# A graph-network kernel whose adjacency loads are merged from two of 2 MB to one of 4 MB

## What is computed

```python
h = relu(layernorm(x))
Wh = h @ W
e = leaky_relu(Wh @ a1 + (Wh @ a2).T, 0.2)
att = softmax(where(adj > 0, e, -9e15), axis=-1)
x = x + relu(att @ Wh)
h = relu(layernorm(x))
node = h @ W1
hw = einsum('nc,kcf->nkf', h, W2)
y = adj @ einsum('nk,nkf->nf', node, hw)
out = x + relu(y + node @ b)
```

## Time and profile before

| | |
|---|---|
| median of 3 runs | 1871.63 us (1871.55 to 1872.37) |
| profiled execution, device time | 1872.76 us |
| its span, first to last instruction | 1871.2 us |
| PE busy | 98% of the span |
| ACT, DVE, POOL busy | 71%, 65%, 38% |
| moved by DMA | 452 MB, 242 GB/s over the span |
| mean granted clock of TensorE | 0.993 of full speed |

### The profile page before, as it was taken

One profiled execution on the slowest core, in us unless ns is written; L12 is line 12 of the kernel. 1 busy time (PEld: TensorE's weight loads), 2 busy tenths in 40 slices (PEclk: granted clock), 3 DMA queues, 4 the chain that ended last, 5 costly groups with the idle time before them and its releaser, 6 DMA issues.

```text
span 1871.2 us, 38399 instructions
## 1 busy us (share of the span) xinstructions
PE 1831.2 (98%) x13404; PEld 1590.1 (85%) x13404; DVE 1209.9 (65%) x1511; ACT 1330.3 (71%) x2144; POOL 714.5 (38%) x530
## 2 busy tenths in 40 slices
PE   7799999999999999999999999999999999999998
PEld 4699989889889888988988888898877788888886
DVE  6666677677767767777776776776656543443534
ACT  4666788877878787887788778878465655555554
POOL 0300056546546655654665564565535400000000
PEclk9899999999999999999999999999999999999999
DMA  9488967776776776777777677674753344445430
GB/s 332 154 311 320 352 243 283 289 276 265 287 288 251 295 290 251 288 284 274 271 287 278 263 292 280 251 295 156 309 198 144 141 161 161 154 159 205 152 157 22
DMA packets 105812, 452.24 MB, mean 242 GB/s; under 512 B 6736, under 2 KB 15136, under 8 KB 87968
## 3 DMA queue, kind: packets, MB, share of 16 engines
q1 hardware_dynamic: 86720, 356.53, 51.2%
q10 hardware_dynamic: 12208, 75.62, 9.9%
q0 software_dynamic: 6832, 19.41, 2.8%
HBM read 364.46 MB, written 87.07 MB: 241 GB/s over the span
## 4 chain that ended last, share of the span: by engine, by line
PE 91%; DVE 3%; ACT 2%; issue 2%; SPq 1%; DMA 1%; DVEq 0%; ACTq 0%
PE ot_ps L806 47%; PE mt_ps L850 13%; PE ot_ps L850 13%; PE hw_ps L770 11%; PE mt_ps L738 6%; ACT wh_mask L505 1%; PE h_ps L765 1%; DVE att L947 1%; DMA adj_sb<-in_adj_dram 1%; SPq L283 1%; DVE p_sb L971 1%; DVE p_sb L897 1%; ACT prod L571 1%; DVE keep L952 0%; PE h_ps L777 0%
## 5 line engine op out<-in xcount | busy, mean ns | idle before, releaser
L806 PE MATMUL ot_ps<-wh_mask,p_sb 128*128 (+1 forms) x8192 | 980.6, 277 | 5.8 <-DVE p_sb L971 5.8
L971 DVE SCALAR_TENSOR_TENSOR p_sb<-zb,qcol,mt 128x1024 f32<-128x1024 uint8 (+1 forms) x512 | 780.6, 1555 | 263.3 <-ACT mt L517 212.2
L806 PEld LDWEIGHTS ot_ps<-wh_mask,p_sb 128*128 128x128 f32 x8192 | 942.3, 192 | 7.7 <-issue 5.9
L378 POOL TENSOR_TENSOR prod<-prod 128x1024 f32<-128x1024 f32 (+2 forms) x192 | 408.0, 2125 | 516.5 <-ACT prod L571 500.6
L505 ACT ACTIVATE wh_mask<-adj_sb 128x2048 uint8<-128x2048 f32 x256 | 492.9, 1928 | 3.3 <-DMA adj_sb<-in_adj_dram 2.2
L632 ACT ACTIVATE mask<-adj_sb 128x1024 fp32r<-128x1024 uint8 x240 | 255.4, 1065 | 176.5 <-PE ot_ps L850 176.4
L517 ACT ACTIVATE mt<-mt_ps 128x1024 uint16<-128x1024 uint16 x256 | 267.5, 1046 | 151.8 <-PE mt_ps L738 150.5
L1009 DVE CAST mask<-adj_sb 128x1024 fp32r<-128x1024 uint8 x272 | 202.3, 750 | 248.5 <-PE mt_ps L850 246.6
L571 ACT ACTIVATE prod<-hw_ps,node 128x128 f32<-128x128 f32 x1024 | 278.8, 385 | 92.1 <-PE hw_ps L770 92.1
L850 PE MATMUL mt_ps<-mask,msgs 128*128 128x512 f32 x1024 | 283.0, 398 | 4.3 <-issue 3.4
L850 PE MATMUL ot_ps<-mask,msgs 128*128 128x512 f32 x1024 | 275.6, 391 | 0.8
(11 more groups left out here) (112 smaller groups left out, 612.5 us busy)
## 6 DMA issues: line engine op xcount, KB each, us to landing
adj_sb<-in_adj_dram SPq DMA_DIRECT2D x128, 2048.0 KB, 8.4
maskT_d<-mt ACTq DMA_DIRECT2D x64, 1024.0 KB, 5.2
adj_sb<-maskT_d SPq DMA_DIRECT2D x32, 2048.0 KB, 7.7
keep_d<-keep POOLq DMA_DIRECT2D x64, 128.0 KB, 6.0
p_sb<-keep_d SPq DMA_DIRECT2D x4, 2048.0 KB, 12.2
msg_d<-msg POOLq DMA_DIRECT2D x56, 128.0 KB, 5.9
msgs<-msg_d SPq DMA_DIRECT2D x7, 1024.0 KB, 10.2
wh_mask<-in_x_dram SPq DMA_DIRECT2D x8, 512.0 KB, 7.3
```

The lines of the kernel that those rows point to most:

```text
L378: pool.tensor_tensor(prod[:, 0:n, :], prod[:, 0:n, :], prod[:, n:2 * n, :], ALU.add)\
L806: ins = pe.matmul(ot_ps[h][:, (t - t0) * ROW:(t - t0 + 1) * ROW], p_sb[:, r, t * P:(t + 1) * P], rows, start=False, stop=end and t == t1 - 1)
L971: dve.scalar_tensor_tensor(p_sb[:, r, :], zbf[:, bass.ds((ib % 2) * BLK, BLK)], qcol[:, bass.ds(tile + b_, 1)], mtb[:, p, k, :, b_], ALU.m ...
```

## The change

The two loads of a half turn become one. SP waits until both quarters of the half have been cast, then issues one load of all eight rows per partition (4 MB) into both quarters; it raises one semaphore, `adj_in[p]`, and all four casts of the half wait for that one. The casts, their order, `adj_cast`, and everything behind them are as before. `past_sp` is a semaphore that nothing waits for; the increment only separates two waits on SP.

```diff
--- before.py
+++ after.py
@@ -185,7 +185,7 @@
         z0_copied = sem("z0_copied")
         z_stored = sem("z_stored")
         zb_in = sem("zb_in")
-        adj_in = [sem(f"adj_in{q}") for q in range(4)]
+        adj_in = [sem("adj_in0"), sem("adj_in1")]
         adj_cast = [sem(f"adj_cast{q}") for q in range(4)]
         turned = sem("turned")
         evicted = sem("evicted")
@@ -287,12 +287,12 @@
             def turn(i, ib, jg, finish, last):
                 for p in range(2):
                     for h in range(2):
-                        q = 2 * p + h
-                        sp.wait_ge(adj_cast[q], i)
-                        sp.dma_start(adj_sb[:, q, :].rearrange("p (t n) -> p t n", n=BLK),
-                                     adj_v[bass.ds(ib, 1), :, h * HT:(h + 1) * HT,
-                                           bass.ds((2 * jg + p) * BLK, BLK)].rearrange("i p t n -> (i p) t n"))\
-                          .then_inc(adj_in[q], 16)
+                        sp.wait_ge(adj_cast[2 * p + h], i)
+                        sp.sem_inc(past_sp, 1)
+                    sp.dma_start(adj_sb[:, 2 * p:2 * p + 2, :].rearrange("p h n -> p (h n)")
+                                 .rearrange("p (t n) -> p t n", n=BLK),
+                                 adj_v[bass.ds(ib, 1), :, :, bass.ds((2 * jg + p) * BLK, BLK)]
+                                 .rearrange("i p t n -> (i p) t n")).then_inc(adj_in[p], 16)
 
             attention_loop(sp, turn)
 
@@ -499,7 +499,7 @@
 
             def cast(q, part, count, turned_before):
 
-                act.wait_ge(adj_in[q], 16 * count)
+                act.wait_ge(adj_in[q // 2], 16 * count)
                 act.wait_ge(turned, turned_before)
                 t = q % 2 * HT + part * (HT // 2)
                 ins = act.activation(m8[:, q // 2, t:t + HT // 2, :].rearrange("p t n -> p (t n)"),
```

## The result

| | before | changed |
|---|---|---|
| median | 1871.97 us (6 runs, 1871.55 to 1872.57) | 1879.12 us (6 runs, 1877.34 to 1880.01) |
| ratio to before | | 1.0037, 95% interval 1.0024 to 1.0050 |
| span of the profiled execution | 1871.2 us | 1875.8 us |

The change makes the kernel 7.15 us slower, 0.37%. The forecast was 1876.7 us, or 4.7 us above that median. The profiled execution of the changed kernel is its fastest run (1877.34 us); a second set of runs, further down, has a profile nearer to its median.

The account below looks back on a forecast made before the run. The prediction took PE to bound the kernel (busy 98% of the span, 91% of the chain). Its terms, +5.1 + 0 + 0 + 0 on the median 1871.63, gave 1876.7 us, range 1872.8 to 1883.

Parts of the forecast that it names:

- The first load: At the start, the first cast waits for all 4 MB, landing at 34.2 us in place of 29.1: +5.1 us.
- That nothing absorbs it: Behind the first cast, everything is waiting, so the 5.1 us delay arrives at the end whole.
- The clock: PE's clock behind the first wait and at the start of attention: 3.84 us won or lost as bounds, taken as 0.
- The rival by which the clock gives the delay back: At the start of attention and the step after the wait, full clock returns 3.84 us: 1872.9 us, not slower; chance 0.23.
- Loads in block 0: Attention loads in block 0 take 15.5 us of the 18.3 us available, 2.8 us to spare, so cost 0.
- the 12.5 to 16 us that the prediction named: Sign for the profile after: loads should land in 12.5 to 16 us.
- its own sign, that ACT waits for a load after 82 us: During attention, the prediction called itself wrong if ACT waits for a load after 82 us.
- the loads of attention: Loads in blocks 0 to 7 fit between issue and need: 15.5 of 18.3 us, later 16.3 of 21.5; cost 0.
- Less traffic in the way: Fewer, longer loads leave gaps for small stores; PE could win 4.3 us over blocks 1 to 7, 1868.6 us; chance 0.03.
- A late load at the end of block 0: Rival: block 0 loads over 18.3 us stall ACT, 4.9 us late at 23.2, up to 14.7 us in all; chance 0.08.

Follow-up runs that it names:

- second set of runs: The changed kernel run and profiled again, nothing altered: 1879.84 us (5 runs) against 1872.58 for the kernel before, ratio 1.0041.
- The kernel with nothing else changed: The kernel before with only the two half turns of the first turn loaded as 4 MB, other loads at 2 MB: 1877.53 us against 1872.17.
- with all of the costs of the change removed: The changed kernel with the first turn at 2 MB loads, first xt load before attention, start casts one step later: 1869.35 us, ratio 0.9984 to before.
- The store of 128 KB: The changed kernel with mask stores and their third-stage loads cut to 16 of 128 partitions; result wrong, kernel time no measure; 4 MB load 13.2 us.

## Why the prediction was right, and where not

**The first load: right.** The working gave +5.1 us for the first cast; it is +4.66 (33.80 - 29.14) in the profile after and +4.87 in the second one. The load itself took 18.3 us, as worked out (34.2 - 15.9); it was issued a little earlier, at 15.5 and 15.7. The kernel with nothing else changed gave +5.36 us in time. To read the cost from the landing of the second load was sound.

**That nothing absorbs it: right.** PE's first attention matmul is 4.08 us late in the first profile, 4.74 in the second (86.90), and 5.04 with only the first turn merged (87.20). The casts one step later show it from the other side: where there is work in front of the wait, the wait shrinks. One reading of the lines was wrong, without harm to the sum: DVE's 4.10 us and PE's 3.24 us of idle time end at 31.27 and 31.96 us, behind the cast, and not when the load lands. At 29.14 us DVE had been idle for 2.0 us and PE for 0.4. They were idle, though, and that is all the argument needs.

**The clock: near the middle of its bounds, as taken.** The step behind the first cast took 7.00 and 7.46 us, against 7.59 before, and 7.64 with only the first turn merged (41.76 - 34.12). With the old wait it is 7.64 again in the kernel with the first turn split. So the longer idle time of PE did not make it worse by anything that shows. Two windows of the changed kernel (busy us of the five engines, granted clock, DMA share, GB/s):

```profile
34.00:40.00 6.00, 3.38 (x18) 3.41 (x19) 4.00 (x19) 3.55 (x7) 0.00 (x0) 0.54 1.02 409
...
82.00:88.00 6.00, 3.68 (x19) 2.93 (x20) 6.00 (x3) 3.48 (x6) 6.00 (x4) 0.66 0.04 8
```

The clock is 0.54 behind the long wait, so nearly all of that stretch is at 1.2 GHz; before, it was 0.87 from 29 to 34 us and 0.82 from 34 to 40. The step is none the longer for it. PE works for 3.38 of those 6 us, so part of the low clock falls on idle time. Ahead of the first attention matmuls it is 0.66, and they take 5.97 us against 6.31. The rival by which the clock gives the delay back won 0.6 + 0.3 us in the first profile and 0.1 + 0.1 in the second, of the 1.4 it needed; it did not decide.

**Loads in block 0: the term was mis-sized.** I took 15.5 us for a load; the median is 16.9. The error is in the step where a mask store beside the load adds half of 5.1 us: it adds 3.7. As there were 18.3 us of room the conclusion held for the median, with 1.4 us to spare and not 2.8. Of the eight loads issued in block 0 after the start two took longer than 18.3 us: the first, 20.1, which nobody waited for, and the last, 20.7, with `xt` and a load of 512 KB into `zb` beside it. The last was 0.78 us late. No load of attention landed within the 12.5 to 16 us that the prediction named; the fastest took 16.2. And by its own sign, that ACT waits for a load after 82 us, the prediction is wrong in this step. The second profile has no such wait.

**The step that failed is the list of who is late next.** For the loads of attention I checked each against its own deadline and wrote a cost of 0. I did not ask what a load twice as long does to the transfers beside it, though the list of DMA issues in the trace has them, `xt` among them. The mask store went from 5.2 to 10.0 us and `xt` from 6.6 to 12.5, and `xt` had only one place with less room than that: the head of block 1, behind the short half turns of block 0. It had 218.20 - 207.68 = 10.5 us of room there and took 13.3. Of the 7.15 us, 5.1 were foreseen; the first load's part measured 0.3 more, the loads of attention 1.4 where I had 0, and 0.4 is more than the two parts make alone, which is within the intervals.

**The rivals.** Less traffic in the way did not make anything faster: with all of the costs of the change removed it equals the kernel before. A late load at the end of block 0 came once in the first profile, for 0.78 us, not at all in the second, and never for 4.9.

## What to carry to other kernels

Merging two transfers moves their readiness to that of the later one, and where a pipeline starts, everything waits for the first of them; read the price from the landing of the second transfer, and ask first whether some work can be put in front of the wait. When a transfer gets longer or is issued in a lump, check the deadlines of the other transfers and not only its own: the one with the least room between issue and use decides, however small it is. A wait that is gone can be gained only once, so two cures for it are not worth more than one.

## What the runs showed of the hardware

Three things I had not expected. A load of 4 MB takes 13.2 us nearly alone and 16.9 with a store of 1 MB beside it, which is more than the store's share of bytes. And a store of 1 MB, issued when up to 4 MB of loads are outstanding, takes 10 us in place of 5, whether those are one transfer of 4 MB (10.0) or two of 2 MB (9.8): what counts is how many bytes are being moved beside it, not how they were asked for. The third is where the store loses its time. The Trainium skill says that each DMA engine goes round the queues packet by packet (DMA: Bandwidth & Descriptors, "Queues, rings and completion order"). The packets of ACT's queue and of SP's (number, MB, share of 16 engines) from 152 to 153 us in the changed kernel agree, if one goes by the profile's packets:

```profile
q10 hardware_dynamic: 33, 0.27, 65.1%
q1 hardware_dynamic: 33, 0.14, 35.1%
```

Each queue moves 33 packets, the store's of 8 KB and the load's of 4 KB, so the store gets two thirds of the bytes. With three queues at work, from 221 to 222 us, they move 37, 37 and 34. With equal bytes instead, the store would be through when as much of the load has gone: an estimated 7 us, from 5.1 us for 2 MB and that page's fixed part of 2 (which it states for transfers issued from GpSimd). The runs have 10, and not because the turns go against the store. This store was issued at 146.80 us, and the first packet of its queue is on record near 151.3, 4.5 us later. The store of 128 KB waits 3.5 us in the same way. In the kernel before, where the load beside it is nearly through, it is 0.7 to 1.1 us. So a store issued behind a large outstanding load starts late, the full one and the small one alike, and then has its turns. What fills the time before its first packet, in which the engines are busy and move 254 to 266 GB/s, the profile does not show.
